# Eight transposes of a softmax tile in one PSUM tile, with one high and one low copy of it

## The chip, the core and the metric

The kernel runs on one core of a Trainium2 chip. The metric is device time in microseconds (us), from one launch of the whole program; the kernel before was timed three times. A profile is one more execution, recorded by the hardware profiler. The engines that matter are TensorE (PE; PEld is its weight load), VectorE (DVE), ScalarE (ACT), GpSimd (POOL) and SyncE (SP), which starts the loads. Each works its own instructions in order and waits on semaphores for the others.

## What is computed

The reference is a chain of four blocks on x of shape 2 x 512 x 1024: a cross attention, a router mixture, a fake-quantised product and a feed-forward block with 4-bit weights. The change lies in the attention alone. Cut to that, it is:

```python
q = (query @ wq).reshape(bs, sq, 32, 128).transpose((0, 2, 1, 3))
k = repeat of (key @ wk), 8 heads to 32        # 1024 keys
v = repeat of (value @ wv), 8 heads to 32
q = _apply_rope(q, 0); k = _apply_rope(k, 0)
raw = jnp.einsum('bhqd,bhkd->bhqk', q, k) / scale
masked = raw + mask
attn = jax.nn.softmax(masked, axis=-1)
out = jnp.einsum('bhqk,bhkd->bhqd', attn, v)
```

## The kernel before

The program is a row of stages, with a barrier between them. `attention_stage` (tile names begin with `at_`) reads rotated Q, K and projected V from scratch in HBM and writes the attention output back. Its unit of work is a step: 128 queries of one head against all 1024 keys. There are 2 batches x 32 heads x 4 steps = 256 steps, and they run in a software pipeline over all engines. Products are done in split precision: each operand is a high part in fp32r and a low part (the value less the high part), and `split_matmul` (L117 to L119) adds three products.

For step n the work passes through these places:

- TensorE, `scores`: six matmuls into the PSUM tile `at_s` (two buffers).
- VectorE, `mask_and_max` (L940, L941, L944): adds the mask, takes the row maximum, and writes `at_sc`.
- ScalarE, `exponentials` (L888): `at_pr` = exp(`at_sc` - max), with the row sum.
- VectorE, `normalise` (L948, L950), one step later: `at_pr` times one over the sum.
- TensorE, `turn` (L991), two steps behind the scores: eight 128x128 transposes of `at_pr` into the PSUM tile `at_t`. This tile has two halves of four transposes (one PSUM bank each). It has no second buffer.
- ScalarE, `turn_high` (L898): copies each half of `at_t` to `at_pth`, the high part.
- VectorE, `turn_low` (L957): for each half, `at_t` less the high part goes to `at_ptl`.
- TensorE, `mix`, six steps behind the scores: six of the 24 matmuls of a head, V times the transposed weights, into `at_o`.

What sets the order is written out in `do_step` of each engine. In step n, TensorE issues scores(n), turn(n-2) and mix(n-6). VectorE does mask_and_max(n), normalise(n-1) and turn_low(n-2). ScalarE first does what `fetches` names for this step (the high part of a new Q, K or V), then turn_high(n-2) and exponentials(n), and once in four steps the copy of a head's output. GpSimd takes the low parts of Q (L853, 128x512, once in four steps), K (L847) and V (L850, both 128x1024, each once in sixteen steps: at n = 8 and n = 10 modulo 16); it starts each when ScalarE's high part of it is done.

Semaphores are counters. `event.free(n, ring)` is the count at which the use of a buffer `ring` uses back has ended. `turned`, `t_hi` and `t_lo` count halves, two a step. In `turn`, TensorE waits for `normed` and, ahead of each half, for `t_lo` of the same half of the step before:

```python
for j in range(2):
    pe.wait_ge(t_lo.sem, t_lo.free(2 * step(b, i, n) + j, 2))
    for c in range(HALF):
        k = j * HALF + c
        last = pe.transpose(t_ps[:, j, c, :], pr[:, n % 2, k * P:(k + 1) * P], ident[:])
    last.then_inc(turned.sem, 1)
```

The stage is emitted with hardware loops (`Fori`) of 32 steps a pass, with some steps written out ahead and behind.

Of the kernel before, what the change touches and what calls it, by code (L numbers as in the profile page):

```python
# [22 lines left out]
ACT = mybir.ActivationFunctionType  # L23
AX = mybir.AxisListType

P = 128
# [6 lines left out]
KT = SK // P  # L33
QT = SQ // P
# [75 lines left out]
def f32(ap):  # L110

    return ap.bitcast(F32)
# [605 lines left out]
def attention_stage(nc, q_d, k_d, v_d, o_d, mask, ident):  # L718
# [8 lines left out]
    with ExitStack() as ctx:  # L727
        sb, ps, sem, event = make_tools(ctx, nc, "at")
# [1 line left out]
        HP = KG * GRP  # L730
        NS = HP * QT
        PASSES = HKV // KG
        HALF = KT // 2

        mk = sb("mk", [P, B * QT, SK], F32)
        kraw = sb("kraw", [P, SK], F32)
# [6 lines left out]
        pr = sb("pr", [P, 2, SK], F32)  # L743
# [2 lines left out]
        sm = sb("sm", [P, 2, 4], F32)  # L746
        turnstile = sb("turnstile", [P, 1], F32)
        s_ps = ps("s", [P, 2, SK])
        t_ps = ps("t", [P, 2, HALF, P])
        o_ps = ps("o", [P, 2, SQ])  # L750

        mask_in, k_in, v_in = sem("mask_in"), sem("k_in"), sem("v_in")
# [8 lines left out]
        expd = event("expd", 2)  # L761
        recipd = event("recipd")
        normed = event("normed")
        turned = event("turned", 4)
        t_hi = event("t_hi")
        t_lo = event("t_lo", 2)
        mixed = event("mixed", HP)
        copied = event("copied", 2)
        block = ctx.enter_context(nc.Block())
# [5 lines left out]
        def head(b, i, h):  # L775
            return i * HP + (b * HQ + h)

        def step(b, i, n):
            return i * NS + (b * HQ * QT + n)
# [86 lines left out]
        @block.scalar  # L866
        def _(act):
            def fetch(b, i, kind, x):
                if kind == "k":

                    act.wait_ge(k_in, group(b, i, x) * 16 + 16)
                    act.wait_ge(scored.sem, scored.free(step(b, i, (x + 1) * GRP * QT - 1), NS))
                    act.activation(kk[0][:, x % KG], kraw[:], ACT.Copy).then_inc(k_hi.sem, 1)
                elif kind == "v":

                    act.wait_ge(v_in, group(b, i, x) * 16 + 16)
                    act.wait_ge(mixed.sem, mixed.free(head(b, i, (x + 1) * GRP - 1), HP))
                    act.activation(vv[0][:, x % KG], vraw[:], ACT.Copy).then_inc(v_hi.sem, 1)
                else:

                    act.wait_ge(q_in[x % 2], i * (16 * HP // 2) + 16 * (b * HQ // 2 + x // 2 + 1))
                    act.wait_ge(scored.sem, scored.free(step(b, i, QT * (x + 1) - 1), 2 * QT))
                    act.activation(qq[0][:, x % 2], qraw[:, x % 2], ACT.Copy).then_inc(q_hi.sem, 1)  # L883

            def exponentials(b, i, n):
                act.wait_ge(maxed.sem, maxed.done(step(b, i, n)))
                act.wait_ge(turned.sem, turned.free(2 * step(b, i, n) + 1, 4))
                act.activation(pr[:, n % 2], sc[:, n % 2], ACT.Exp, bias=sm[:, n % 2, 1:2],  # L888
                               accum_out=sm[:, n % 2, 2:3]).then_inc(expd.sem, 1)

            def turn_high(b, i, n):
                h = n // QT
                if n % QT == 0:

                    act.wait_ge(mixed.sem, mixed.free(head(b, i, h), 2))
                for j in range(2):
                    act.wait_ge(turned.sem, turned.done(2 * step(b, i, n) + j))
                    act.activation(pt[0][:, h % 2, j * HALF:(j + 1) * HALF, (n % QT) * P:(n % QT + 1) * P],  # L898
                                   t_ps[:, j], ACT.Copy).then_inc(t_hi.sem, 1)

            def copy_out(b, i, h):
                act.wait_ge(mixed.sem, mixed.done(head(b, i, h)))
                act.wait_ge(o_st[h % 2], i * (16 * HP // 2) + 16 * (b * HQ // 2 + h // 2 + 1))
                act.activation(ot[:, h % 2], o_ps[:, h % 2], ACT.Copy).then_inc(copied.sem, 1)

            def store_out(b, i, h):
                bb, hh = at(b, i, h)
                act.wait_ge(copied.sem, copied.done(head(b, i, h)))
                act.dma_start(o_d[bass.ds(hh, 1)].rearrange("a p n -> p (a n)")[:, bb * SQ:(bb + 1) * SQ],
                              ot[:, h % 2]).then_inc(o_st[h % 2], 16)  # L910

            def do_step(b, i, n):
                for kind, x in fetches(b, i, n):
                    fetch(b, i, kind, x)
                if exists(b, i, n - 2):
                    turn_high(b, i, n - 2)
                if exists(b, i, n):
                    exponentials(b, i, n)
                for lag, act_on in ((COPY_LAG, copy_out), (STORE_LAG, store_out)):
                    if (n - lag) % QT == 0 and exists(b, i, n - lag):  # L920
                        act_on(b, i, (n - lag) // QT)

            expd.open(act)
            copied.open(act)
            for s in range(2):
                act.sem_inc(o_st[s], 16)
            for kind, x in FIRST:
                fetch(0, 0, kind, x)
            program(act, do_step)
            for s in range(2):  # L930
                act.wait_ge(o_st[s], 16 * (B * HQ // 2 + 1))

        @block.vector
        def _(dve):
# [16 lines left out]

            def turn_low(b, i, n):
                h = n // QT
                for j in range(2):
                    sl = (slice(None), h % 2, slice(j * HALF, (j + 1) * HALF), slice((n % QT) * P, (n % QT + 1) * P))
                    dve.wait_ge(t_hi.sem, t_hi.done(2 * step(b, i, n) + j))
                    dve.tensor_tensor(pt[1][sl], t_ps[:, j], f32(pt[0][sl]), ALU.subtract).then_inc(t_lo.sem, 1)  # L957

            def do_step(b, i, n):
                for lag, act_on in ((0, mask_and_max), (1, normalise), (2, turn_low)):  # L960
# [9 lines left out]
        def _(pe):  # L970
# [13 lines left out]

            def turn(b, i, n):
                pe.wait_ge(normed.sem, normed.done(step(b, i, n)))
                for j in range(2):
                    pe.wait_ge(t_lo.sem, t_lo.free(2 * step(b, i, n) + j, 2))
                    for c in range(HALF):
                        k = j * HALF + c  # L990
                        last = pe.transpose(t_ps[:, j, c, :], pr[:, n % 2, k * P:(k + 1) * P], ident[:])  # L991
                    last.then_inc(turned.sem, 1)

            def mix(b, i, n):

                h, quarter = n // QT, n % QT
                g = h // GRP
                if h % GRP == 0 and quarter == 0:
                    pe.wait_ge(v_lo.sem, v_lo.done(group(b, i, g)))
                if quarter == 0:  # L1000
                    pe.wait_ge(t_lo.sem, t_lo.done(2 * step(b, i, QT * (h + 1) - 1) + 1))
                    pe.wait_ge(copied.sem, copied.free(head(b, i, h), 2))
                for c in share(KT, quarter, QT):
                    last = split_matmul(pe, o_ps[:, h % 2], [x[:, g % KG, c, :] for x in vv],
                                        [x[:, h % 2, c, :] for x in pt], c == 0, c == KT - 1)
                if quarter == QT - 1:
                    last.then_inc(mixed.sem, 1)
# [949 lines left out]
```

## Time and profile before

| | us |
|---|---|
| median of three runs | 3843.18 |
| lowest, highest | 3840.72, 3857.33 |
| span of the profiled execution | 3848.1 |
| TensorE busy in it | 3119.9 (81%) |
| VectorE busy in it | 3251.7 (85%) |
| ScalarE busy in it | 2177.6 (57%) |
| GpSimd busy in it | 1180.3 (31%) |

The busy shares are means over stages that have different limits. The attention stage lies between about 1240 and 2220 us of the span, and the views below are taken from it. A timeline row gives the start of an instruction (or a run of equal ones), how long it lasts, the engine, the line, output and inputs, and in brackets how long the engine sat idle before it and for whom. A run of several (x2, x8) lasts from the start of the first to the end of the last, and neighbours overlap, since the engines start one before the other is written out.

### The profile page before, as it was taken

The page shows a single profiled execution, that of the slowest core. Times are in us where ns is not written, and L with a number is a line of the kernel's source. Part 1 is how long each engine was busy: PE and PEld are TensorE (multiplying, and loading weights), DVE is VectorE, ACT ScalarE, POOL GpSimd, SP SyncE. Part 2 cuts the span into 40 slices and gives each one's busy share as a digit, 9 for nine tenths or more (in the row PEclk, how much of TensorE's full clock was granted, in tenths as well). Part 3 has the DMA queues.
Part 4 walks back from the last instruction along what each step waited for, and adds up shares of the span by engine and source line. Part 5 has one row for each costly group of instructions (what it writes and reads, how often), then busy time and mean ns, then how long its engine had stood idle before and what let it go on. Part 6 is the DMA issues. An engine that isn't in the chain of part 4 may idle for free. (4 is left out here: it accounts for less than half of the span.)

```text
span 3848.1 us, 45676 instructions
## 1 busy us (share of the span) xinstructions
PE 3119.9 (81%) x14144; PEld 2487.0 (65%) x14144; DVE 3251.7 (85%) x4335; ACT 2177.6 (57%) x2742; POOL 1180.3 (31%) x547
## 2 busy tenths in 40 slices
PE   5767665767766999999999977777574699999999
PEld 4555554546645788888888855555442577777787
DVE  7999997877977899999999979999947488878853
ACT  4555554546556677777777655666513265555531
POOL 3777774741732111111111135545100001101000
PEclk8888886889878999999999989989856799999999
DMA  3222223324222211111111032222002212121211
GB/s 107 79 93 71 98 71 103 105 89 142 87 90 93 89 53 52 57 52 54 56 47 58 28 137 98 96 89 87 22 6 88 66 61 77 60 82 61 71 55 52
DMA packets 170336, 286.81 MB, mean 75 GB/s; under 512 B 11712, under 2 KB 98752, under 8 KB 170176
## 3 DMA queue, kind: packets, MB, share of 16 engines
q1 hardware_dynamic: 160960, 268.24, 20.9%
q10 hardware_dynamic: 9216, 16.78, 1.2%
q8 instruction: 58, 0.95, 0.1%
q14 instruction: 102, 0.84, 0.1%
HBM read 196.64 MB, written 88.34 MB: 74 GB/s over the span
## 5 line engine op out<-in xcount | busy, mean ns | idle before, releaser
L220 DVE SCALAR_TENSOR_TENSOR pq_nf_val<-pq_nf_above,pq_nf_val 128x1024 f32<-128x1024 f32 x224 | 449.3, 2006 | 10.2
L898 ACT ACTIVATE at_pth<-at_t 128x512 fp32r<-128x512 f32 x512 | 281.9, 596 | 249.5 <-PE at_t L991 249.5
L205 ACT ACTIVATE pq_nf_above<-pq_nf_raw,sharp 128x1024 f32<-128x1024 f32 x240 | 273.7, 1148 | 256.6 <-DVE pq_nf_val L220 255.1
L220 DVE SCALAR_TENSOR_TENSOR ou_nf_val<-ou_nf_above,ou_nf_val 128x1024 f32<-128x1024 f32 x224 | 395.1, 1764 | 5.8
L205 ACT ACTIVATE ou_nf_above<-ou_nf_raw,sharp 128x1024 f32<-128x1024 f32 x240 | 274.6, 1150 | 197.9 <-DVE ou_nf_val L220 184.3
L117 PE MATMUL pq_pj<-xT_h,pq_wh 128*128 128x512 f32 x512 | 227.4, 444 | 180.1 <-POOL pq_wl L483 180.1
L941 DVE CUSTOM_DVE_ANT_0 at_sc<-at_s,at_mk 128x1024 f32<-128x1024 f32 x256 | 312.1, 1219 | 60.4 <-issue 35.2
L205 ACT ACTIVATE ff_nf_above<-ff_nf_raw,sharp 128x1024 f32<-128x1024 f32 x255 | 291.7, 1148 | 92.4 <-DVE ff_nf_val L220 72.8
L957 DVE TENSOR_TENSOR at_ptl<-at_t,at_pth 128x512 fp32r<-128x512 f32 x512 | 328.0, 682 | 1.1 <-ACT at_pth L898 1.1
L117 PE MATMUL ou_acc<-ou_wh,ou_oh 128*128 128x512 f32 x512 | 225.2, 440 | 127.9 <-DVE X L1158 110.1
L220 DVE SCALAR_TENSOR_TENSOR ff_nf_val<-ff_nf_above,ff_nf_val 128x1024 f32<-128x1024 f32 x238 | 308.0, 1294 | 21.2 <-ACT ff_nf_above L205 18.6
L888 ACT ACTIVATE at_pr<-at_sc,at_sm 128x1024 f32<-128x1024 f32 x256 | 295.3, 1154 | 21.9 <-DVE at_sm L944 15.2
L117 PE MATMUL ff_g<-yT_h,ff_guh 128*128 128x512 f32 x704 | 286.8, 407 | 0.0
L991 PE MATMUL at_t<-ident,at_pr 128*128 128x128 f32 x2048 | 272.8, 274 | 16.6 <-DVE at_ptl L957 16.6
L991 PEld LDWEIGHTS at_t<-ident,at_pr 128*128 128x128 f32 x2048 | 235.2, 140 | 67.6 <-DVE at_ptl L957 28.0
L119 PE MATMUL ff_g<-yT_h,ff_gul 128*128 128x512 f32 x704 | 276.5, 393 | 0.0
L118 PE MATMUL ff_g<-yT_l,ff_guh 128*128 128x512 f32 x704 | 274.8, 390 | 0.0
L853 POOL TENSOR_TENSOR at_ql<-at_qraw,at_qh 128x512 fp32r<-128x512 f32 x64 | 82.3, 1285 | 576.4 <-ACT at_qh L883 576.4
L197 POOL TENSOR_TENSOR ff_nf_raw<-ff_nf_raw,ff_nf_am 128x1024 f32<-128x1024 f32 x17 | 39.5, 2321 | 692.4 <-DVE ff_nf_am L192 692.4
L117 PEld LDWEIGHTS pq_pj<-xT_h,pq_wh 128*128 128x128 f32 x512 | 110.3, 215 | 217.1 <-DVE pq_tb L463 119.7
L117 PE MATMUL at_s<-at_kh,at_qh 128*128 128x512 f32 x512 | 201.5, 393 | 32.5 <-POOL at_ql L853 26.9
L950 DVE TENSOR_SCALAR at_pr<-at_pr,at_sm 128x1024 f32<-128x1024 f32 x256 | 219.0, 855 | 9.1
(210 smaller groups left out, 8710.5 us busy)
## 6 DMA issues: line engine op xcount, KB each, us to landing
ff_raw<-dq SPq DMA_DIRECT2D x63, 512.0 KB, 4.0
pq_raw<-in_L_xattn_wq SPq DMA_DIRECT2D x32, 512.0 KB, 5.0
q_d<-pq_res SPq DMA_DIRECT2D x32, 512.0 KB, 2.6
at_qraw<-q_d SPq DMA_DIRECT2D x64, 256.0 KB, 2.7
o_d<-at_ot ACTq DMA_DIRECT2D x64, 256.0 KB, 2.0
ou_oraw<-o_d SPq DMA_DIRECT2D x32, 512.0 KB, 3.4
ou_wraw<-in_L_xattn_wo SPq DMA_DIRECT2D x32, 512.0 KB, 3.5
pq_nf_raw<-in_L_ffn_w SPq DMA_DIRECT2D x16, 512.0 KB, 5.4
```

What stands on the lines that cost most here:

```text
L117: pe.matmul(out, w[0], x[0], start=start, stop=False)
L118: pe.matmul(out, w[0], x[1], start=False, stop=False)
L119: return pe.matmul(out, w[1], x[0], start=False, stop=stop)
L205: act.activation(self.above[:, (s + j) % 2, 0:width], self.raw[:, s, 0:width], ACT.Relu, bias=self.sharp[:, j:j + 1], scale=SHARP).then_in ...
L220: dve.scalar_tensor_tensor(v, above, STEPS[j], v, ALU.min, ALU.add).then_inc(self.stepped.sem, 1)
L853: pool.tensor_tensor(qq[1][:, x % 2], qraw[:, x % 2], f32(qq[0][:, x % 2]), ALU.subtract).then_inc(q_lo.sem, 1)
L888: act.activation(pr[:, n % 2], sc[:, n % 2], ACT.Exp, bias=sm[:, n % 2, 1:2], accum_out=sm[:, n % 2, 2:3]).then_inc(expd.sem, 1)
L898: act.activation(pt[0][:, h % 2, j * HALF:(j + 1) * HALF, (n % QT) * P:(n % QT + 1) * P], t_ps[:, j], ACT.Copy).then_inc(t_hi.sem, 1)
L941: dve.tensor_tensor_reduce(sc[:, n % 2], s_ps[:, n % 2], mk[:, bb * QT + n % QT], 1.0, NEG, ALU.add, ALU.max, sm[:, n % 2, 0:1]).then_inc( ...
L950: dve.tensor_scalar(pr[:, n % 2], pr[:, n % 2], sm[:, n % 2, 3:4], None, ALU.mult).then_inc(normed.sem, 1)
L957: dve.tensor_tensor(pt[1][sl], t_ps[:, j], f32(pt[0][sl]), ALU.subtract).then_inc(t_lo.sem, 1)
L991: last = pe.transpose(t_ps[:, j, c, :], pr[:, n % 2, k * P:(k + 1) * P], ident[:])
```

## The change

The tile `at_t` is declared as one block of eight transposes rather than two halves. It takes the same two PSUM banks. `turned`, `t_hi` and `t_lo` count steps, one each. TensorE waits once, for the whole low part of the step before, and signals once after its eighth transpose. ScalarE's high copy and VectorE's subtraction are one 128x1024 instruction each. The exponential of step n still waits for the transposes of step n-2, and the mix for the last low part of its head.

```diff
-        t_ps = ps("t", [P, 2, HALF, P])
+        t_ps = ps("t", [P, KT, P])
...
-        turned = event("turned", 4)
+        turned = event("turned", 2)
         t_hi = event("t_hi")
-        t_lo = event("t_lo", 2)
+        t_lo = event("t_lo", 1)
...
-                act.wait_ge(turned.sem, turned.free(2 * step(b, i, n) + 1, 4))
+                act.wait_ge(turned.sem, turned.free(step(b, i, n), 2))
...
-                for j in range(2):
-                    act.wait_ge(turned.sem, turned.done(2 * step(b, i, n) + j))
-                    act.activation(pt[0][:, h % 2, j * HALF:(j + 1) * HALF, (n % QT) * P:(n % QT + 1) * P],
-                                   t_ps[:, j], ACT.Copy).then_inc(t_hi.sem, 1)
+                act.wait_ge(turned.sem, turned.done(step(b, i, n)))
+                act.activation(pt[0][:, h % 2, :, (n % QT) * P:(n % QT + 1) * P], t_ps[:], ACT.Copy).then_inc(t_hi.sem, 1)
...
-                for j in range(2):
-                    sl = (slice(None), h % 2, slice(j * HALF, (j + 1) * HALF), slice((n % QT) * P, (n % QT + 1) * P))
-                    dve.wait_ge(t_hi.sem, t_hi.done(2 * step(b, i, n) + j))
-                    dve.tensor_tensor(pt[1][sl], t_ps[:, j], f32(pt[0][sl]), ALU.subtract).then_inc(t_lo.sem, 1)
+                sl = (slice(None), h % 2, slice(None), slice((n % QT) * P, (n % QT + 1) * P))
+                dve.wait_ge(t_hi.sem, t_hi.done(step(b, i, n)))
+                dve.tensor_tensor(pt[1][sl], t_ps[:], f32(pt[0][sl]), ALU.subtract).then_inc(t_lo.sem, 1)
...
-                for j in range(2):
-                    pe.wait_ge(t_lo.sem, t_lo.free(2 * step(b, i, n) + j, 2))
-                    for c in range(HALF):
-                        k = j * HALF + c
-                        last = pe.transpose(t_ps[:, j, c, :], pr[:, n % 2, k * P:(k + 1) * P], ident[:])
-                    last.then_inc(turned.sem, 1)
+                pe.wait_ge(t_lo.sem, t_lo.free(step(b, i, n), 1))
+                for k in range(KT):
+                    last = pe.transpose(t_ps[:, k, :], pr[:, n % 2, k * P:(k + 1) * P], ident[:])
+                last.then_inc(turned.sem, 1)
...
-                    pe.wait_ge(t_lo.sem, t_lo.done(2 * step(b, i, QT * (h + 1) - 1) + 1))
+                    pe.wait_ge(t_lo.sem, t_lo.done(step(b, i, QT * (h + 1) - 1)))
```

On TensorE, one step of the stage's start in the program before (scores, then the transposes of two steps back; the names in brackets are the semaphores waited for):

```order
L117 MATMUL at_s<-at_kh,at_qh 128x512 [waits at_masked]
L118 MATMUL at_s<-at_kl,at_qh 128x512
L119 MATMUL at_s<-at_kh,at_ql 128x512
...
L991 MATMUL at_t<-ident,at_pr 128x128 [waits at_t_lo,at_normed]
L991 MATMUL at_t<-ident,at_pr 128x128 x3
L991 MATMUL at_t<-ident,at_pr 128x128 [waits at_t_lo]
L991 MATMUL at_t<-ident,at_pr 128x128 x3
```

The same place in the changed program (L985 is the line that was L991):

```order
L117 MATMUL at_s<-at_kh,at_qh 128x512 [waits at_masked]
L118 MATMUL at_s<-at_kl,at_qh 128x512
L119 MATMUL at_s<-at_kh,at_ql 128x512
...
L985 MATMUL at_t<-ident,at_pr 128x128 [waits at_t_lo,at_normed]
L985 MATMUL at_t<-ident,at_pr 128x128 x7
```

The order of work is the same. One of the two waits on `at_t_lo` is gone, and the one that is left asks for the whole tile.

## Rows read from the trace of the kernel before

**Rows 1.** Windows: busy us and instructions of each engine, clock, DMA.

```profile
core 0: us, PE busy (x) PEld busy (x) DVE busy (x) ACT busy (x) POOL busy (x), PEclk, DMA share, GB/s
1240.00:2220.00 980.00, 944.39 (x5120) 787.24 (x5120) 894.68 (x2048) 692.75 (x1185) 159.04 (x96) 0.99 0.17 56
1540.00:1550.00 10.00, 8.55 (x46) 6.83 (x45) 8.57 (x22) 6.22 (x12) 1.29 (x1) 1.00 0.22 77
```

**Rows 2.** Timeline of one ordinary step: start, us, engine, line, tile.

```profile
1599.83 1.03 PE L991 MATMUL at_t<-ident,at_pr 128*128 128x128 f32 x8
1600.03 1.22 DVE L941 CUSTOM_DVE_ANT_0 at_sc<-at_s,at_mk 128x1024 f32<-128x1024 f32 x1
1600.46 1.09 ACT L898 ACTIVATE at_pth<-at_t 128x512 fp32r<-128x512 f32 x2 [1.23 <-PE at_t L991]
1601.57 1.15 ACT L888 ACTIVATE at_pr<-at_sc,at_sm 128x1024 f32<-128x1024 f32 x1
1602.22 1.28 DVE L957 TENSOR_TENSOR at_ptl<-at_t,at_pth 128x512 fp32r<-128x512 f32 x2
...
1603.21 1.02 PEld L991 LDWEIGHTS at_t<-ident,at_pr 128*128 128x128 f32 x8
1603.41 1.28 POOL L853 TENSOR_TENSOR at_ql<-at_qraw,at_qh 128x512 fp32r<-128x512 f32 x1 [8.63 <-ACT at_qh L883]
1603.44 1.03 PE L991 MATMUL at_t<-ident,at_pr 128*128 128x128 f32 x8
1603.65 1.22 DVE L941 CUSTOM_DVE_ANT_0 at_sc<-at_s,at_mk 128x1024 f32<-128x1024 f32 x1
...
1605.17 0.75 DVE L950 TENSOR_SCALAR at_pr<-at_pr,at_sm 128x1024 f32<-128x1024 f32 x1
```

**Rows 3.** Waits in the stage: who waited for whom, us, times, longest.

```profile
PEld at_t L991 <- DVE at_ptl L957: 28.0, 56, 1.9
```

**Rows 4.** Timeline of a K step (L847 is GpSimd's K low part).

```profile
1642.46 1.04 ACT L873 ACTIVATE at_kh<-at_kraw 128x1024 fp32r<-128x1024 f32 x1
1643.19 1.03 PE L991 MATMUL at_t<-ident,at_pr 128*128 128x128 f32 x8
1643.39 1.22 DVE L941 CUSTOM_DVE_ANT_0 at_sc<-at_s,at_mk 128x1024 f32<-128x1024 f32 x1
1643.58 2.41 POOL L847 TENSOR_TENSOR at_kl<-at_kraw,at_kh 128x1024 fp32r<-128x1024 f32 x1 [9.98 <-ACT at_kh L873]
1644.92 1.62 DVE L950 TENSOR_SCALAR at_pr<-at_pr,at_sm 128x1024 f32<-128x1024 f32 x1
1646.46 1.27 DVE L957 TENSOR_TENSOR at_ptl<-at_t,at_pth 128x512 fp32r<-128x512 f32 x2
1647.19 0.42 PEld L991 LDWEIGHTS at_t<-ident,at_pr 128*128 128x128 f32 x4 [0.66 <-DVE at_ptl L957]
...
1651.03 1.03 PE L991 MATMUL at_t<-ident,at_pr 128*128 128x128 f32 x8
```

**Rows 5.** Groups of the stage: busy us, mean ns, idle before.

```profile
L957 DVE TENSOR_TENSOR at_ptl<-at_t,at_pth 128x512 fp32r<-128x512 f32 x512 | 328.0, 682 | 1.1 <-ACT at_pth L898 1.1
L941 DVE CUSTOM_DVE_ANT_0 at_sc<-at_s,at_mk 128x1024 f32<-128x1024 f32 x256 | 312.1, 1219 | 60.4 <-issue 35.2
L898 ACT ACTIVATE at_pth<-at_t 128x512 fp32r<-128x512 f32 x512 | 281.9, 596 | 249.5 <-PE at_t L991 249.5
L950 DVE TENSOR_SCALAR at_pr<-at_pr,at_sm 128x1024 f32<-128x1024 f32 x256 | 219.0, 855 | 9.1
```

**Rows 6.** Timeline of the step behind a loop's branch.

```profile
1541.11 0.06 DVE L940 MEMSET at_turnstile<- 128x1 f32 x1 [2.10 <-issue]
...
1543.38 1.28 DVE L957 TENSOR_TENSOR at_ptl<-at_t,at_pth 128x512 fp32r<-128x512 f32 x2
1544.12 0.42 PEld L991 LDWEIGHTS at_t<-ident,at_pr 128*128 128x128 f32 x4 [1.87 <-DVE at_ptl L957]
...
1544.72 0.42 PEld L991 LDWEIGHTS at_t<-ident,at_pr 128*128 128x128 f32 x4 [0.18 <-DVE at_ptl L957]
```

More of the change, by code:

```diff
@@ L732, in attention_stage @@
         PASSES = HKV // KG
-        HALF = KT // 2
         mk = sb("mk", [P, B * QT, SK], F32)
```

## The prediction

> **What bounds the kernel now.** I read the busy table over the attention stage first: of 980 us TensorE is busy 944.39 and VectorE 894.68 at a granted clock of 0.99 [rows 1]. So TensorE sets the pace, VectorE follows at 91%, and ScalarE (692.75) and GpSimd (159.04) have room. Nothing outside the stage is touched. Then the timeline of one ordinary step shows who waits for whom [rows 2]. I measure from the start of VectorE's masked maximum (L941), called T. T is 1600.03 and the next one is at 1603.65, so a step takes 3.61 to 3.62 us; I use 3.61. In that step:
> - the pair of low parts (L957) starts at 1602.22 = T + 2.19 and ends at 1603.50 = T + 3.47; its first half ends at 1602.22 + 0.68 = T + 2.87;
> - TensorE loads weights for the next step's transposes at 1603.21 = T + 3.18 and multiplies from 1603.44 = T + 3.41, with no wait;
> - the next T comes 0.21 after that multiply starts (1603.65 - 1603.44), because the scores are issued just ahead of the transposes.
>
> The reader is to see this: at T + 3.18 the first half of the tile has been free for 0.3 us, but the second half is not free until T + 3.47. The transposes of the first half cover the gap. That cover is what the change takes away.
>
> **The kinds of steps.** The waits view puts most of TensorE's waiting in the stage on L957: 28.0 us in 56 waits before weight loads [rows 3]. They belong to two kinds of step. In the first, GpSimd takes a K or V low part. Its 128x1024 subtraction runs 1643.58 to 1645.99, and the normalise (L950) that starts at 1644.92 lasts 1.62 instead of 0.75, ending at 1646.54, 0.55 after GpSimd's end [rows 2, 4]. I read this as VectorE standing until GpSimd is through, so that the end of a long normalise follows GpSimd's end. Their number: L950 is busy 219.0 us where 256 x 0.75 would be 192, and 27 / 0.87 is about 31 [rows 5]; it fits the 16 K and 16 V groups less the pair that is loaded ahead of the first step, so 30. There the low pair starts at 1646.46 = T + 3.07, and TensorE loses 0.46 on the first half (load at 1647.19, multiply some 0.07 later at 1647.26, where 1643.19 + 3.61 = 1646.80 was due) and 0.15 on the second (next transposes at 1651.03, not 1647.26 + 3.61) [rows 4]. So 0.61 us for each of 30. In the second kind, four steps after a loop's branch, VectorE stands 2.10 us on issue and the loads follow 1.87 us late [rows 6].
>
> **The change, part by part.**
> Fewer instructions: 256 copies on ScalarE and 256 subtractions on VectorE go. A 512-element low part lasts 682 ns and a copy 596 [rows 5], but a pair lasts only 1.28 and 1.09, as the second overlaps the first [rows 2]. No single 128x1024 of these two lines is in the trace. For the low part the nearest row is L941, 1219 ns for 1024 elements with a PSUM source [rows 5], so I take 1.22; the bounds are 1.15 and the pair's own 1.28. For the copy the nearest is the K copy, 1.04 [rows 4]; I take 1.03, bounds 1.02 and the pair's 1.09. That saves about 0.06 us a step on each engine. Worth at most 0.06 x 256 = 15 us if VectorE were the bound; TensorE is, so I book zero. TensorE's own instructions stay the same.
>
> The wait on the whole tile, ordinary step: TensorE may load only when the one low part has ended, T + 2.19 + 1.22 = T + 3.41, plus 0.05 for the handoff (1646.46 + 0.68 = 1647.14, load at 1647.19 [rows 4]): T + 3.46 where it was T + 3.18. The multiply no longer trails its load by 0.23 but by 0.07, so it starts at T + 3.53 where it was T + 3.41. Late by 0.12. Behind the waiting load stand this step's output products and the next scores, and VectorE waits for those. But this step's T was set by the scores ahead of the wait, so the lateness reaches the wait again only two steps on: one lap is 3.61 (transposes to transposes) + 0.21 (to T) + 3.53 = 7.35 us for two steps against 7.22, 0.13 per two steps. I expect periods of 3.61 and 3.74 in turn. Steps in K or V pairs aside, 256 - 60 = 196 steps are 98 laps: 98 x 0.13 = 12.7 us.
>
> The same wait, K and V steps: here a second effect adds. ScalarE's copy now starts after eight transposes, not four. It started 0.63 after the first transpose (1600.46 - 1599.83). The eight transposes last 1.03 [rows 2]; with 0.03 for the handoff it will start at 1.06 and end at 2.09, where the pair ended at 0.63 + 1.09 = 1.72. The exponential behind it, the K or V copy behind that and GpSimd's subtraction all start some 0.35 later against T. GpSimd ends now at T + 2.60 (1645.99 - 1643.39 [rows 4]), so then at T + 2.60 + 0.35 = T + 2.95, the normalise ends 0.55 later at T + 3.50 (about 1.97 long instead of 1.62), and the low part starts 0.09 before that end, as in both timelines, at T + 3.41. It ends at T + 4.63, TensorE loads at T + 4.68 and multiplies at T + 4.75. Due was T - 0.21 + 3.61 = T + 3.40, so 1.35 is lost where 0.61 was: 0.74 x 30 = 22.2 us. Of the 0.74, 0.35 is GpSimd's shift and the rest the missing half.
>
> After the loop's branch: the low pair there starts at 1543.38; now the halves go at 1544.12 and 1544.72 [rows 6], in the new form one load at 1543.38 + 1.22 + 0.05 = 1544.65. Four transposes' time makes up part of it: about 0.38 x 4 = 1.5 us.
>
> Does the copy still arrive in time? In a late step the transposes start at T - 0.08, the copy ends at T + 2.01 and with 0.05 for the handoff is seen at T + 2.06; in the other at T + 1.93. VectorE is free for the low part at T + 2.19. Slack 0.13 to 0.26, so it hides. GpSimd's 1.28 us Q subtraction ends at 1604.69, 0.48 before the normalise at 1605.17 [rows 2], and will end some 0.12 before it: still hidden.
>
> Sum: 12.7 + 22.2 + 1.5 = **36.4 us**. Against the profiled execution, 3848.1 us, that is 3884.5. The three runs have their median at 3843.2, within 4.9 us of it, so the forecast is 3843.2 + 36.4 = **3879.6 us** (+0.95%).
>
> **A rule against the row.** The timeline and the groups show two 512-element low parts in 1.28 us and one operation of 1024 elements in 1.22 [rows 2, 5], a gain of 0.06. The Trainium skill, "Advanced Engine Details and Errata", section The Read-Write Bubble, says that VectorE and ScalarE pay the memory latency between instructions, so that large tiles are to be used, and that one instruction may read several PSUM banks. The trace agrees on the saving but gives it to an engine that is not the bound. The same notes, "Perfetto Trace Analysis", section Optimizing Scalar/DVE Operations, say the reverse for this place: where these engines are not saturated but cause gaps on others, breaking instructions up may help. By the first rule the sum would be about -15 us, by the second a loss.
>
> **The rivals.**
> 1. The ordinary wait vanishes. If the low part takes 1.15, or the hand-over is quicker after a single wait, the 0.13 of a lap is used up. Then K and V steps lose 0.61 more instead of 0.74: 18.3 + about 0.5, so 3862. For it: the lap is late by only 0.13 on sums of five rows. Against it: the steps around it repeat to 0.01 to 0.03.
> 2. The lap grows. If the one copy takes 1.15 like the exponential (L888 [rows 2]) or the handoffs cost 0.1 more, the low part waits for the copy, the slack of 0.13 is gone and each lap gains 0.1 to 0.15 more: 12 us, and 30 x 0.1 = 3 in K and V steps. If GpSimd's Q part then runs into the normalise as well, 60 x 0.05 = 3. Together 3895 to 3900. A fall of the clock would also be here, but in the windows it stays at 1.00 through the 1.87 us wait of the loop branch [rows 1, 6].
> 3. Faster. The wait costs nothing, because TensorE's load is in practice let through as early as now, and VectorE's shorter work counts: 0.06 x 256 = 15 us, plus the second-half wait of 0.15 in 30 K and V steps, 4.5. It gives 3843.2 - 20 = 3823. It decides if the whole low part ends by T + 3.13; with its start at T + 2.19 it would have to take 0.94 us, less than any 1024-element row with a PSUM source.
> 4. No difference: the copies or subtractions are split again when built, or slack that I do not see takes it all: 3843.
>
> **How the numbers follow.** Forecast 0.68 (its bounds, low part 1.15 to 1.28, give +27 to +44, so 3870 to 3887), rival 1 0.13, rival 2 0.13, rival 3 0.03, rival 4 0.03. The range 3858 to 3899 takes in rival 1 and nearly all of rival 2; outside lie rivals 3 and 4 and the tail of rival 2, about 0.1, and the rest is for terms that I mis-sized. About 0.5% (19 us) is what a measurement of this kernel can tell from no change. Rival 1 lies on that edge, so half of it counts as same: faster 0.03, same 0.10, slower 0.87.
>
> **What would show it right or wrong.** In the profile after, the attention stage should be 36 us longer and everything else equal. Periods between masked maxima should be 3.61 and 3.74 in turn; equal periods of 3.61 mean rival 1. Long normalises should be near 1.97 us, and the K and V steps should show TensorE waits of about 1.3 us, 30 of them; long normalises still at 1.62 would take 0.35 x 30 = 10.5 us off. The low part's row should read 1.22 and the copy's 1.03; a copy near 1.15 means rival 2. TensorE busy unchanged, its share of the stage down from 96 to 93%.

## The result, and the profile after

The changed kernel takes 3894.81 us (median of four runs, 3888.43 to 3900.10) against 3846.89 for the kernel before, measured beside it. The ratio is 1.0115 with a 95% interval of 1.0092 to 1.0139, so it is 35 to 53 us slower, 44 by the ratio (the two medians differ by 47.9). The forecast was +36.4 us, 3879.6, with a range of 3858 to 3899: 15.2 us below the measured median, of which 3.7 are the kernel before, whose own median moved from 3843.18 to 3846.89. The span of the profiled execution went from 3848.1 to 3886.6, +38.5.

The windows view shows the attention stage of the changed kernel (us, then busy time and instructions of TensorE, its weight loads, VectorE, ScalarE and GpSimd, then clock, DMA share and GB/s); it answers to [rows 1]:

```profile
core 0: us, PE busy (x) PEld busy (x) DVE busy (x) ACT busy (x) POOL busy (x), PEclk, DMA share, GB/s
1240.00:2262.00 1022.00, 959.08 (x5120) 777.16 (x5120) 889.05 (x1792) 648.33 (x929) 158.89 (x96) 0.99 0.16 54
```

TensorE has the same 5120 matmuls at the same clock of 0.99, in 1022 us instead of 982 (before, the same stretch ends at 2222). Its busy time rose from 944.39 to 959.08 us all the same. A matmul's record lasts 0.39 us while the next one starts 0.23 after it, so a short delay of the next one is filled by the tail of the record and counts as busy. Busy time hides part of this loss. From the first masked maximum to the last the stage takes 983.9 us where it took 943.9: +40.0. I call this the stage's length below. The rest of the span is 2902.8 against 2904.2. VectorE and ScalarE are busy for less time, not more (889 against 895, 648 against 693): what was saved on them was not on the path.

The groups of the stage, against [rows 5]:

```profile
L953 DVE TENSOR_TENSOR at_ptl<-at_t,at_pth 128x1024 fp32r<-128x1024 f32 x256 | 311.9, 1218 | 8.7 <-ACT at_pth L896 5.0
L896 ACT ACTIVATE at_pth<-at_t 128x1024 fp32r<-128x1024 f32 x256 | 263.1, 1028 | 345.9 <-PE at_t L985 345.9
L947 DVE TENSOR_SCALAR at_pr<-at_pr,at_sm 128x1024 f32<-128x1024 f32 x256 | 225.7, 881 | 10.6 <-DVE at_sm L945 1.6
```

The one subtraction lasts 1218 ns and the one copy 1028, as I had taken them (1.22 and 1.03). The normalise, whose code is the same, costs 6.7 us more, since it stands longer behind GpSimd.

The waits view, against [rows 3]:

```profile
PEld at_t L985 <- issue: 109.9, 218, 2.8
PE at_t L985 <- DVE at_ptl L953: 44.0, 42, 2.4
```

Before there were 56 such waits ahead of a weight load, in special steps. Now there are 218, in nearly every step. Most are put down to issue, that is to no releaser, because the wait that holds them up does not stand on the load itself (see the eighth run).

Two ordinary steps and a bit more of the timeline, for [rows 2]:

```profile
1636.83 1.22 DVE L938 CUSTOM_DVE_ANT_0 at_sc<-at_s,at_mk 128x1024 f32<-128x1024 f32 x1 [0.23 <-issue]
1637.85 1.03 ACT L896 ACTIVATE at_pth<-at_t 128x1024 fp32r<-128x1024 f32 x1 [1.12 <-PE at_t L985]
1639.02 1.22 DVE L953 TENSOR_TENSOR at_ptl<-at_t,at_pth 128x1024 fp32r<-128x1024 f32 x1
1640.36 0.86 PEld L985 LDWEIGHTS at_t<-ident,at_pr 128*128 128x128 f32 x8 [0.20 <-issue]
1640.63 1.22 DVE L938 CUSTOM_DVE_ANT_0 at_sc<-at_s,at_mk 128x1024 f32<-128x1024 f32 x1 [0.39 <-issue]
...
1642.82 1.22 DVE L953 TENSOR_TENSOR at_ptl<-at_t,at_pth 128x1024 fp32r<-128x1024 f32 x1
1644.16 0.86 PEld L985 LDWEIGHTS at_t<-ident,at_pr 128*128 128x128 f32 x8 [0.38 <-issue]
1644.24 1.22 DVE L938 CUSTOM_DVE_ANT_0 at_sc<-at_s,at_mk 128x1024 f32<-128x1024 f32 x1 [0.20 <-issue]
...
1648.07 1.22 DVE L938 CUSTOM_DVE_ANT_0 at_sc<-at_s,at_mk 128x1024 f32<-128x1024 f32 x1 [0.42 <-issue]
```

The masked maxima (L938, formerly L941) follow each other after 3.80, 3.61 and 3.83 us: the forecast's long and short period in turn, where every period was 3.61. The weight load comes 0.12 us after the subtraction's end (1642.82 + 1.22 = 1644.04, load at 1644.16). The forecast had 0.05 for that. What lies between the two is one instruction of TensorE's queue for weight loads. The source view of line L983, over this same stretch of 1640 to 1644.5 us, shows it:

```profile
L983 PEldq EVENT_SEMAPHORE  x2: 51/51/51, 1640.3 to 1644.1; - x2
```

It does nothing but wait for a semaphore, starts when the subtraction has ended, and is recorded with 51 ns. The weight load follows it.

A K step with three rows of the step before it, for [rows 4]:

```profile
1659.16 1.22 DVE L938 CUSTOM_DVE_ANT_0 at_sc<-at_s,at_mk 128x1024 f32<-128x1024 f32 x1 [0.23 <-issue]
1660.17 1.03 ACT L896 ACTIVATE at_pth<-at_t 128x1024 fp32r<-128x1024 f32 x1 [1.15 <-PE at_t L985]
1661.10 1.15 ACT L887 ACTIVATE at_pr<-at_sc,at_sm 128x1024 f32<-128x1024 f32 x1
...
1662.93 1.22 DVE L938 CUSTOM_DVE_ANT_0 at_sc<-at_s,at_mk 128x1024 f32<-128x1024 f32 x1 [0.37 <-issue]
1663.36 2.41 POOL L846 TENSOR_TENSOR at_kl<-at_kraw,at_kh 128x1024 fp32r<-128x1024 f32 x1 [10.39 <-ACT at_kh L872]
1664.45 1.86 DVE L947 TENSOR_SCALAR at_pr<-at_pr,at_sm 128x1024 f32<-128x1024 f32 x1
1666.23 1.21 DVE L953 TENSOR_TENSOR at_ptl<-at_t,at_pth 128x1024 fp32r<-128x1024 f32 x1
1667.38 1.21 DVE L938 CUSTOM_DVE_ANT_0 at_sc<-at_s,at_mk 128x1024 f32<-128x1024 f32 x1
1667.56 0.86 PEld L985 LDWEIGHTS at_t<-ident,at_pr 128*128 128x128 f32 x8 [1.45 <-issue]
```

GpSimd starts 0.43 after the maximum instead of 0.19, the normalise lasts 1.86 instead of 1.62 and ends 0.54 after GpSimd, and TensorE's load comes after 1.45 us of idle time on its own queue. With the step behind it, a K or V pair takes 8.52 us (medians 4.42 and 4.10 for K and for V) where it took 7.87.

### The profile page after: what moved, and what is told of

The parts are those of the page before. It is cut to its first block and busy times, and to the rows that moved or that the text cites. A ratio compares the mean times of both kernels' runs of the same rounds, so it can differ in the third digit from the quotient of the medians.

```text
span 3886.6 us, 44164 instructions
## 1 busy us (share of the span) xinstructions
PE 3120.3 (80%) x14140; PEld 2468.3 (64%) x14144; DVE 3239.4 (83%) x4079; ACT 2133.1 (55%) x2486; POOL 1181.6 (30%) x547
## 5 line engine op out<-in xcount | busy, mean ns | idle before, releaser
L896 ACT ACTIVATE at_pth<-at_t 128x1024 fp32r<-128x1024 f32 x256 | 263.1, 1028 | 345.9 <-PE at_t L985 345.9
L938 DVE CUSTOM_DVE_ANT_0 at_sc<-at_s,at_mk 128x1024 f32<-128x1024 f32 x256 | 312.1, 1219 | 101.8 <-issue 101.7
L953 DVE TENSOR_TENSOR at_ptl<-at_t,at_pth 128x1024 fp32r<-128x1024 f32 x256 | 311.9, 1218 | 8.7 <-ACT at_pth L896 5.0
L985 PE MATMUL at_t<-ident,at_pr 128*128 128x128 f32 x2048 | 270.5, 275 | 44.0 <-DVE at_ptl L953 44.0
L985 PEld LDWEIGHTS at_t<-ident,at_pr 128*128 128x128 f32 x2048 | 224.6, 141 | 115.1 <-issue 109.9
L947 DVE TENSOR_SCALAR at_pr<-at_pr,at_sm 128x1024 f32<-128x1024 f32 x256 | 225.7, 881 | 10.6 <-DVE at_sm L945 1.6
```

Of the source, the lines that this page charges most:

```text
L896: act.activation(pt[0][:, h % 2, :, (n % QT) * P:(n % QT + 1) * P], t_ps[:], ACT.Copy).then_inc(t_hi.sem, 1)
L938: dve.tensor_tensor_reduce(sc[:, n % 2], s_ps[:, n % 2], mk[:, bb * QT + n % QT], 1.0, NEG, ALU.add, ALU.max, sm[:, n % 2, 0:1]).then_inc( ...
L947: dve.tensor_scalar(pr[:, n % 2], pr[:, n % 2], sm[:, n % 2, 3:4], None, ALU.mult).then_inc(normed.sem, 1)
L953: dve.tensor_tensor(pt[1][sl], t_ps[:], f32(pt[0][sl]), ALU.subtract).then_inc(t_lo.sem, 1)
L985: last = pe.transpose(t_ps[:, k, :], pr[:, n % 2, k * P:(k + 1) * P], ident[:])
```

## The experiments

Each kernel was profiled, timed in three rounds beside the kernel before, and its stage measured in its own trace. A lap is two ordinary steps, a pair a K or V step and the one behind it; both are added up from the median period of each of the sixteen steps in which the pattern repeats. The rest of the program, in which these kernels do not differ, took between 2896.8 and 2913.8 us in the profiled executions. So the stage's length tells apart what the total time cannot, and I judge by it. It comes from one execution each, and the steps behind a loop's branch alone move it by up to 10 us between kernels, so where it and the laps and pairs disagree, the laps and pairs are the firmer figures.

| kernel | stage, us | over before | lap | K/V pair | ratio of times (95%) |
|---|---|---|---|---|---|
| before | 943.9 | | 7.23 | 7.87 | |
| changed | 983.9 | +40.0 | 7.44 | 8.52 | 1.0115 (1.0092 to 1.0139) |
| 1, whole wait only | 973.5 | +29.6 | 7.45 | 8.14 | 1.0067 (1.0050 to 1.0083) |
| 2, whole copy only | 946.2 | +2.3 | 7.23 | 8.10 | 0.9999 (0.9985 to 1.0012) |
| 3, whole wait and low part | 973.8 | +29.9 | 7.42 | 8.15 | 1.0074 (1.0057 to 1.0091) |
| 4, before, K/V in halves | 927.3 | -16.6 | 7.23 | 7.24 | 0.9953 (0.9931 to 0.9975) |
| 5, changed, K/V in halves | 952.9 | +9.1 | 7.43 | 7.43 | 1.0019 (1.0007 to 1.0030) |
| 6, changed, mix ahead | 977.5 | +33.6 | 7.34 | 8.53 | 1.0068 (1.0042 to 1.0094) |
| 7, both 5 and 6 | 941.4 | -2.5 | 7.34 | 7.34 | 0.9995 (0.9981 to 1.0009) |
| 8, changed, counters apart | 972.4 | +28.5 | 7.38 | 8.46 | 1.0066 (1.0049 to 1.0083) |

**1. Only the wait.** The kernel before, with TensorE asking for the whole tile:

```diff
                 for j in range(2):
-                    pe.wait_ge(t_lo.sem, t_lo.free(2 * step(b, i, n) + j, 2))
+                    if j == 0:
+                        pe.wait_ge(t_lo.sem, t_lo.free(2 * step(b, i, n) + 1, 2))
```

> The kernel before, with one edit: TensorE waits ahead of the first transpose for both halves of the last low part. Copies and subtractions stay in halves. Theory A (the loss is the wait for the whole tile): the pair of low parts ends at T+3.47, the hand-over takes 0.05 to 0.12 and the multiply starts 0.06 later, so a lap of two steps is 7.41 to 7.48 us instead of 7.22, 19 to 25 us over 98 laps; a K or V step loses about 1.1 instead of 0.61, 15 us over 30. Together the attention stage is 32 to 40 us longer than before, nearly the whole loss of the change. Long normalises stay at 1.62 to 1.67. Theory B (the loss comes from the longer instructions, which deliver late): 0 to 5 us.

Measured: +29.6 us, under the 32 to 40 expected, and the lap is 7.45 against the changed kernel's 7.44. Its timeline, first inside a hardware loop and then in the written-out steps:

```profile
1642.01 1.28 DVE L957 TENSOR_TENSOR at_ptl<-at_t,at_pth 128x512 fp32r<-128x512 f32 x2
1643.35 0.86 PEld L992 LDWEIGHTS at_t<-ident,at_pr 128*128 128x128 f32 x8 [0.39 <-DVE at_ptl L957]
1643.43 1.22 DVE L941 CUSTOM_DVE_ANT_0 at_sc<-at_s,at_mk 128x1024 f32<-128x1024 f32 x1
1647.25 1.22 DVE L941 CUSTOM_DVE_ANT_0 at_sc<-at_s,at_mk 128x1024 f32<-128x1024 f32 x1 [0.35 <-issue]
...
1691.77 1.28 DVE L957 TENSOR_TENSOR at_ptl<-at_t,at_pth 128x512 fp32r<-128x512 f32 x2
1693.17 0.87 PEld L992 LDWEIGHTS at_t<-ident,at_pr 128*128 128x128 f32 x8 [0.19 <-issue]
```

So three quarters of the loss come with the wait alone, while every copy and subtraction is still in halves (29.6 of 40.0, each with some branch steps in it: four here, three in the changed kernel). Theory B falls. Two things I did not expect. The K and V pair lost 0.27 over before, not 0.5: long normalises here last 1.46, shorter than before, because the maximum of that step is itself late after a wait while GpSimd is not: GpSimd starts 0.03 after it in the median, where it was 0.19 before. And the hand-over is 0.06 in the first pair of rows (1642.01 + 1.28 = 1643.29, load 1643.35) and 0.12 in the second (1693.05, load 1693.17). The eighth run takes that up.

**2. Only the copy.** The kernel before with one high copy after the eighth transpose, and the subtractions in halves:

```diff
...
-                for j in range(2):
-                    act.wait_ge(turned.sem, turned.done(2 * step(b, i, n) + j))
-                    act.activation(pt[0][...], t_ps[:, j], ACT.Copy).then_inc(t_hi.sem, 1)
+                act.wait_ge(turned.sem, turned.done(2 * step(b, i, n) + 1))
+                act.activation(pt[0][...], t_ps[:], ACT.Copy).then_inc(t_hi.sem, 1)
...
```

> The kernel before, with ScalarE's high copy alone made one 128x1024 instruction after the eighth transpose; the subtractions and TensorE's waits stay in halves. Theory A: ordinary steps stay at 3.61; the K and V subtractions on GpSimd start about 0.23 us later against the normalise, which then lasts about 1.85, so 30 x 0.23 = 7 us longer than before. Theory B: the late copy holds up the low part in every step, 30 us or more.

Ordinary steps keep their lap and the normalise behind GpSimd lasts 1.83, as Theory A had it. The K and V pairs cost 0.23 each more, 7 us over 30. The stage is only 2.3 us longer because none of its steps took over 5 us, while before four did, by some 2 us each, behind a loop's branch. With these 8 us taken off the kernel before, the difference is 10 us, of which the pairs are 7; the other 3 are not accounted for. The group of the normalise:

```profile
L948 DVE TENSOR_SCALAR at_pr<-at_pr,at_sm 128x1024 f32<-128x1024 f32 x256 | 225.7, 882 | 9.1
```

225.7 us is the changed kernel's figure too: the copy's shape alone is enough to give the 6.7 us of standing behind GpSimd.

**3. The low part whole, the copy in halves.**

```diff
...
-                act.wait_ge(turned.sem, turned.done(step(b, i, n)))
-                act.activation(pt[0][...], t_ps[:], ACT.Copy).then_inc(t_hi.sem, 1)
+                for j in range(2):
+                    hs = slice(j * HALF, (j + 1) * HALF)
+                    act.wait_ge(turned.sem, turned.done(2 * step(b, i, n) + j))
+                    act.activation(pt[0][:, h % 2, hs, ...], t_ps[:, hs], ACT.Copy).then_inc(t_hi.sem, 1)
...
```

> The changed kernel, with ScalarE's high copy taken back to two halves; the subtraction and TensorE's wait stay whole. Theory A: a lap of two ordinary steps stays at 7.44 as in the changed kernel (98 x 0.22 = 22 us over before), but GpSimd's K and V parts start as early as before, long normalises are back at about 1.62, and K and V steps lose 0.44 each over before instead of 0.68 (13 us): 35 us over before, 5 to 7 under the changed kernel. Theory B: half of the loss is gone, about 20 us over before.

Measured: +29.9, so 10 us under the changed kernel where 5 to 7 were expected. The lap is 7.42, and the pair lost 0.28, where 0.44 was expected. This execution has five steps over 5 us against three in the changed kernel, so the 10 us are rather too few: by the pairs alone it is 30 x (8.52 - 8.15) = 11. Its K step:

```profile
1656.09 1.22 DVE L942 CUSTOM_DVE_ANT_0 at_sc<-at_s,at_mk 128x1024 f32<-128x1024 f32 x1 [0.34 <-issue]
1656.15 2.40 POOL L847 TENSOR_TENSOR at_kl<-at_kraw,at_kh 128x1024 fp32r<-128x1024 f32 x1 [10.24 <-ACT at_kh L873]
1657.61 1.49 DVE L951 TENSOR_SCALAR at_pr<-at_pr,at_sm 128x1024 f32<-128x1024 f32 x1
1659.02 1.21 DVE L957 TENSOR_TENSOR at_ptl<-at_t,at_pth 128x1024 fp32r<-128x1024 f32 x1
1660.35 0.86 PEld L989 LDWEIGHTS at_t<-ident,at_pr 128*128 128x128 f32 x8 [1.05 <-issue]
```

GpSimd starts 0.06 after the maximum, not 0.43: that is what the halved copy gives back. Runs 1 and 3 have nearly the same length though one has a pair of subtractions and the other a single one. In run 3 the single one ends 0.06 earlier (1.22 against 1.28), and the load comes 0.12 behind it, as in the changed kernel, instead of 0.06: nothing reached TensorE.

**4 and 5. K and V in halves.** The high and low parts of K and V are taken as two pieces of 128x512 each, in steps 8, 10, 11 and 12 of sixteen:

```diff
-            out += [("k", g) for g in [(n + 8) // (GRP * QT)] if g and g * GRP * QT - 8 == n]
-            out += [("v", g) for g in [(n + 6) // (GRP * QT)] if g and g * GRP * QT - 6 == n]
+            for kind, lead in (("k0", 8), ("k1", 6), ("v0", 5), ("v1", 4)):
+                out += [(kind, g) for g in [(n + lead) // (GRP * QT)] if g and g * GRP * QT - lead == n]
...
-                    pool.tensor_tensor(kk[1][:, x % KG], kraw[:], f32(kk[0][:, x % KG]), ALU.subtract).then_inc(k_lo.sem, 1)
+                    last = pool.tensor_tensor(kk[1][:, x % KG, ks], kraw[:, ks], f32(kk[0][:, x % KG, ks]), ALU.subtract)
+                    if part:
+                        last.then_inc(k_lo.sem, 1)
...
```

> The kernel before, with the high and low parts of K and V taken in two halves of 128x512 each, in steps 8, 10, 11 and 12 of sixteen in place of one 128x1024 each in steps 8 and 10. GpSimd's 1.28 us operations should end before the normalise starts. Theory A (the long normalises are VectorE standing behind GpSimd): no normalise over 0.8 us, the 30 K and V stalls of 0.61 vanish, 18 us less than before. Rival: the stall comes from ScalarE's K and V copies ahead of its high copy, or the collision only moves to other steps: 0 to 5 us less.

> The changed kernel with K and V taken in halves as in e4_before_kv. Theory A: only the ordinary laps are left, 127 laps x 0.22 = 28 us over the same kernel in the old form (e4_before_kv), so about 10 us over before. If the K and V steps lost nothing extra by the change, the distance to e4_before_kv would be 40 us.

Run 4 has the first of the four pieces here:

```profile
1636.52 1.28 POOL L851 TENSOR_TENSOR at_kl<-at_kraw,at_kh 128x512 fp32r<-128x512 f32 x1 [9.56 <-ACT at_kh L884]
1636.75 1.22 DVE L953 CUSTOM_DVE_ANT_0 at_sc<-at_s,at_mk 128x1024 f32<-128x1024 f32 x1
1638.27 0.75 DVE L962 TENSOR_SCALAR at_pr<-at_pr,at_sm 128x1024 f32<-128x1024 f32 x1
1638.94 1.28 DVE L969 TENSOR_TENSOR at_ptl<-at_t,at_pth 128x512 fp32r<-128x512 f32 x2
1639.93 1.02 PEld L1003 LDWEIGHTS at_t<-ident,at_pr 128*128 128x128 f32 x8
```

GpSimd is through at 1637.80, before the normalise starts, and the normalise lasts 0.75. The run halves ScalarE's K and V copies as well, so it does not part the two by its total; that the normalise is back at 0.75 speaks for GpSimd. The stage is 16.6 us shorter than before (18 expected), with the median period of each of the sixteen steps at 3.61 to 3.65. Of 256 normalises two still took over 0.8 (0.88 and 0.94), where none was expected to. At a ratio of 0.9953 (0.9931 to 0.9975) this kernel beats both. Run 5 is 25.6 us longer than run 4 (28 expected): with the K and V stalls gone, what the change costs is the lap alone, 7.43 against 7.23. So the 40 us of the change are about 25 for laps over the whole stage, and 14 more that arise only in K and V steps.

**6 and 7. A matmul ahead of the wait.** TensorE issues one matmul of the mix between the scores and the transposes, save in the step where that matmul would wait for the same low part:

```diff
...
-                for lag, act_on in ((0, scores), (2, turn), (MIX_LAG, mix)):
-                    if exists(b, i, n - lag):
-                        act_on(b, i, n - lag)
+                m = n - MIX_LAG
+                ahead = exists(b, i, m) and m % QT != 0
+                if exists(b, i, n):
+                    scores(b, i, n)
+                if ahead:
+                    mix(b, i, m, 0)
+                if exists(b, i, n - 2):
+                    turn(b, i, n - 2)
+                if exists(b, i, m):
+                    mix(b, i, m, 1 if ahead else None)
```

> The changed kernel, with one matmul of the mix (0.227 us of TensorE time) issued between the scores and the transposes, in the three steps of four in which that matmul does not itself wait for the last low part. The order of every sum is the same. Theory A: the wait of an ordinary step (0.22 a lap) is covered by that matmul in these steps, and K and V steps lose 0.2 less: the kernel lies 10 to 20 us over before instead of 40. Periods near 3.61 for three steps in four. Theory B (the time is lost on VectorE or ScalarE, not in TensorE's wait): no change against the changed kernel, 40 us over before.

> The changed kernel with both edits: K and V in halves, and one mix matmul ahead of the transposes in three steps of four. Theory A: nearly all waits of TensorE are covered; it lies within 8 us of e4_before_kv, so 10 to 18 us under before. The loss of the change is then shown to be these two waits alone.

Run 6 missed: 33.6 us over before, not 10 to 20. One half was right. Three periods of four are 3.61 to 3.64 and only the fourth is near 3.80, so the ordinary loss is halved. What remains of it lies in the step left out and in the 0.03 that some covered steps keep. The K and V pairs got nothing back, 8.53. The transposes come later by that matmul, ScalarE with them, and GpSimd with ScalarE:

```profile
1659.55 1.22 DVE L938 CUSTOM_DVE_ANT_0 at_sc<-at_s,at_mk 128x1024 f32<-128x1024 f32 x1 [0.21 <-issue]
1660.21 2.40 POOL L846 TENSOR_TENSOR at_kl<-at_kraw,at_kh 128x1024 fp32r<-128x1024 f32 x1 [10.19 <-ACT at_kh L872]
1661.07 2.09 DVE L947 TENSOR_SCALAR at_pr<-at_pr,at_sm 128x1024 f32<-128x1024 f32 x1
1664.41 0.85 PEld L985 LDWEIGHTS at_t<-ident,at_pr 128*128 128x128 f32 x8 [1.47 <-issue]
```

GpSimd starts 0.66 after the maximum and the normalise lasts 2.09. The cover was paid for in the other stall. In run 7, where that stall does not exist, the same edit takes 11.6 us off run 5 and leaves 14.0 over run 4, where at most 8 was expected: a miss. The step left out explains most of it, since its period is still 3.77 to 3.81 (64 x 0.19 = 12 us). So this run does not show that the two waits are the whole loss, only that what is left stands where TensorE's wait was left uncovered.

**8. Another wait on the load.** Ahead of its first transpose TensorE waits for `t_lo` and for `normed`. The recorded expectation takes it that in the changed kernel one load holds both waits. The semaphores that the trace records with each instruction show otherwise. In the changed kernel, where both counts have the same value, the wait for `t_lo` is the instruction of its own at L983 (256 of them), and the load waits for `normed` alone. In the loops of the kernel before, where the values differ, it is the other way round: the wait for `normed` stands in an instruction ahead, and the load itself waits for `t_lo`. In no trace here does a weight load hold two waits. The run brings the old placing back by letting `t_lo` step by two:

```diff
-        t_lo = event("t_lo", 1)
+        t_lo = event("t_lo", 2)
...
-                dve.tensor_tensor(pt[1][sl], t_ps[:], f32(pt[0][sl]), ALU.subtract).then_inc(t_lo.sem, 1)
+                dve.tensor_tensor(pt[1][sl], t_ps[:], f32(pt[0][sl]), ALU.subtract).then_inc(t_lo.sem, 2)
...
-                pe.wait_ge(t_lo.sem, t_lo.free(step(b, i, n), 1))
+                pe.wait_ge(t_lo.sem, t_lo.free(2 * step(b, i, n) + 1, 2))
...
```

> The changed kernel, with the low part's counter stepping by two a step (as before, when it counted halves) and the waits' values adapted; nothing else. In the hardware loops the wait on the normalise then stands in an instruction of its own ahead, as in the kernel before, and the first weight load waits on one semaphore, not two. Theory A (a load that waits on two semaphores starts 0.11 to 0.12 us after its releaser, one that waits on a single one 0.05): in the 192 steps inside loops the hand-over is 0.05 to 0.06, a lap of two steps is 7.38 instead of 7.44, and the stage is 5 to 6 us shorter than in the changed kernel; in the 64 written-out steps it stays at 0.12. Theory B (the 128x1024 low part itself signals 0.06 later than a 128x512 one): 0.11 to 0.12 everywhere and the stage unchanged at 984 us.

```profile
1638.06 1.22 DVE L953 TENSOR_TENSOR at_ptl<-at_t,at_pth 128x1024 fp32r<-128x1024 f32 x1
1639.33 0.90 PEld L985 LDWEIGHTS at_t<-ident,at_pr 128*128 128x128 f32 x8 [0.17 <-DVE at_ptl L953]
...
1641.82 1.22 DVE L953 TENSOR_TENSOR at_ptl<-at_t,at_pth 128x1024 fp32r<-128x1024 f32 x1
1643.10 0.86 PEld L985 LDWEIGHTS at_t<-ident,at_pr 128*128 128x128 f32 x8 [0.31 <-DVE at_ptl L953]
```

The load is 0.05 and 0.06 behind the subtraction's end (1639.28 and 1643.04). Over the stage, 160 late loads (first loads of a step that have idle time ahead of them in the waits view) have 0.04 to 0.06 and 63, those in written-out steps, 0.11 or 0.12; in the changed kernel all 218 have 0.11 or 0.12. The source view shows where the waits stand, first for this run, then for the kernel before (its L988):

```profile
L983 PEldq FUSED_REGOPS  x192: 37/37/51, 1302.0 to 2156.9; - x192
L983 PEldq EVENT_SEMAPHORE  x64: 51/51/51, 1261.5 to 2239.6; - x64
...
L988 PEldq FUSED_REGOPS  x192: 37/37/51, 1299.3 to 2130.5; - x192
L988 PEldq EVENT_SEMAPHORE  x64: 51/51/51, 1261.2 to 2208.9; - x64
```

The 192 are the steps in loops, where FUSED_REGOPS holds the wait for `normed`, which has long been met, and the load starts on `t_lo` itself. The 64 are the written-out steps, where EVENT_SEMAPHORE holds the wait for `t_lo`. It starts some 0.04 after the subtraction's end and the load 0.07 to 0.08 after its start: together the 0.12. In the changed kernel all 256 have this form.

The lap is 7.38, as expected. Over sixteen steps the medians add up to 61.21 instead of 61.66, 7.2 us for the stage. It is 11.5 us shorter in all, also because this execution had no step over 5 us and the changed kernel's had three. The times and places are those of Theory A and Theory B falls, but the cause that Theory A names does not hold: what costs 0.07 is that the wait that is met last stands in an instruction of its own ahead of the load. It also explains run 1, whose loops still have the load waiting on `t_lo` itself, and why run 3, whose loads do not, gained nothing.

## Why the prediction was right, step by step

- **What bounds the stage, and the lap: right.** TensorE's own work per step did not change. The wait for the whole tile stretched two steps at a time, with long and short periods in turn. Run 1 shows that the wait alone does it.
- **The size of the lap: under.** The step that failed is "plus 0.05 for the handoff". The row it came from was a load that waits for `t_lo` itself; in the changed kernel that wait stands in an instruction ahead of the load, and the hand-over takes 0.12. The written-out steps of the kernel before have that form already, with 0.12 where they are late (eight loads), so this price was in the trace before. The lap is 7.44, not 7.35, and ordinary steps cost about 98 x 0.21 = 20.7 us instead of 12.7 (the medians of twelve ordinary steps add up to 44.6 against 43.4). Run 8 shows 7.2 us of that and of the pairs by itself. With it undone the lap is 7.38, so 0.03 of the difference to 7.35 remains unexplained.
- **K and V steps: right in mechanism, over in size.** 0.65 for each pair, not 0.74: 30 x 0.65 = 19.5 us for 22.2. "All start some 0.35 later against T" was too much; it was 0.24 in the step shown (0.21 in the median). The exponential ahead of it did move by 0.40, from T + 1.54 (1601.57 - 1600.03) to T + 1.94 (1661.10 - 1659.16). But I measured against T as if T stood still, and in a step behind a wait the next T is itself late and takes 0.16 back (3.77 instead of 3.61 here). The exponential also starts 0.10 before the copy's recorded end (1661.10 against 1660.17 + 1.03), which the sum left out. The long normalises are 1.82 to 1.86, not 1.97; the weight loads of these steps come after some 1.45 us of idle time, where I had 1.3. Run 2 shows the shift by itself: 1.83 for the normalise and 0.23 a pair.
- **Durations, and what was booked at zero: right.** 1218 and 1028 ns; neither engine's saving is in the time. "TensorE busy unchanged" did not come out (944.39 to 959.08), but by how records are counted and not by more work. ScalarE's copy and GpSimd's Q part stayed hidden but for one: a single Q part ran into a normalise by 0.1 us near the start.
- **The branch steps: not confirmed.** I had 1.5 us. Four steps over 5 us became three in the changed kernel and none in runs 2 and 8. This term of a few us differs from program to program; I priced it from the one branch step in [rows 6], and nothing there told how many there would be.
- **The sum.** 20.7 + 19.5 is the 40 measured in the stage; 12.7 + 22.2 + 1.5 was the 36.4 forecast. The 44 us of the whole program's times, with an interval of 35 to 53, are consistent with both. The two errors of size, 8.0 too little and 2.7 too much, went opposite ways, so the total looks better than its terms: that part is luck.
- **Rivals.** Rival 1 (no ordinary wait) and rival 3 (faster) fell with the periods of 3.80. Rival 2 named a slower hand-over as one way to a larger lap. That part came true, at 0.07; its other part, the copy at 1.15, did not (1.028). The rule that large tiles save per instruction, from the Trainium skill, "Advanced Engine Details and Errata", section The Read-Write Bubble, holds for VectorE's busy time here (328.0 to 311.9 us) and not for the kernel's. What the Trainium skill says in "Perfetto Trace Analysis", section Optimizing Scalar/DVE Operations, that breaking up instructions may help where these engines make others wait, fits these runs: making the halves whole, and the wait with them, put 40 us on the stage.

## What to carry to other kernels

Where a buffer has no second copy, two halves with a wait each are a second copy in effect: count when each half is asked for, and when it is free, before merging them to save instructions on engines that do not set the pace. When a wait is lengthened, follow the lateness round the loop to where it meets itself, and follow everything queued behind the delayed engine: here 10 to 11 of the 40 us (the changed kernel against run 3) came by ScalarE and GpSimd through a normalise that the change does not touch. Measure the stage in the trace, as the rest of the program varied by 17 us between executions of the same code.

## What was not expected of the hardware

- A weight load whose own wait is the one met last started 0.04 to 0.06 us after its releaser ended (160 late loads in run 8's loops). Where that wait stood in an instruction of its own ahead of the load, it was 0.11 to 0.12 (218 of 218 late loads in the changed kernel). In the loops of these programs the values of two counters decided which of the two waits stood on the load (run 8 changes nothing else), and that alone moved the stage by 7 us. The source view of the wait's line shows it: EVENT_SEMAPHORE or FUSED_REGOPS, and how many.
- A normalise that meets a 2.4 us GpSimd subtraction ended 0.54 to 0.56 us after it, whichever way its start lay (lengths from 1.44 to 2.10 us in these runs). With GpSimd's work cut in pieces that end before it, the K and V stalls are gone (run 4).
- Steps behind a loop's branch took about 2 us more in none (runs 2 and 8), three (the changed kernel), four or five (run 3) steps of the stage, depending on the program. What sets that was not tested and stays open. It is as large as some of the effects studied here.
